# A graph network on one core: the adjacency stage and the gate stage joined in one loop, with one-hots used on chip and sums added up in PSUM

## What is computed

```python
# start of the first layer: the gate of each edge, and its sums by source node
gate = silu(edge_attr @ F1W + F1b) @ F2W + F2b
ei, ej = emb[atom_z[src]], emb[atom_z[dst]]
gate = gate + (ei * (ej @ adapt)).sum(-1, keepdims=True)
cw   = where(distances < CUT, 0.5 * (cos(pi * distances / CUT) + 1.0), 0.0)
mj   = node_mult[dst]
msg  = gate * h[dst] * (cw * mj)[:, None]
agg  = segment_sum(msg, src, num_segments=N)
tot  = clip(segment_sum(mj, src, num_segments=N), 1e-08, None)
h    = _ln(h + agg / tot[:, None], gn, bn)

# later: 5 and 10 steps of m = segment_sum(w * h[row], col)
```

## Time and profile before

| | us |
|---|---|
| median of 3 runs | 9919.12 |
| span of the profiled execution | 10065.2 |
| TensorE matmul busy | 7153.0 (71%) |
| VectorE busy | 6009.4 (60%) |
| GpSimd busy | 4708.2 (47%) |
| ScalarE busy | 3716.3 (37%) |
| stretch of the tables | 1490.0 to 1536.3 |
| adjacency stage | 1536.3 to 2928.4 |
| gate stage with its scans | 2996.7 to 3664.0 |

### The profile page before, as it was taken

How to read it: one execution, slowest core, us unless ns; L and a number is a source line. 1 busy time by engine, 2 the same in 40 slices (tenths; PEclk the granted TensorE clock), 3 DMA queues, 4 the chain that set the end, 5 groups by cost and what they waited for, 6 DMA issues and landing times. The chain is left out here.

```text
span 10065.2 us, 316920 instructions
## 1 busy us (share of the span) xinstructions
PE 7153.0 (71%) x106494; PEld 5756.9 (57%) x106495; DVE 6009.4 (60%) x18492; ACT 3716.3 (37%) x12956; POOL 4708.2 (47%) x6247
## 2 busy tenths in 40 slices
PE   2888865766657849976994998599578788833323
PEld 1555544555547749975994898499434344433323
DVE  6555558888867778997997899799700100011112
ACT  3222216777753326753662676377300000000000
POOL 0777770000016625542551554255267476556665
PEclk9999998888879979987996999799799899855555
DMA  8222224555439949965992997499488899611112
GB/s 330 60 61 61 62 52 162 192 186 188 136 103 308 310 137 255 263 178 147 261 261 65 262 263 205 121 262 263 128 333 334 322 365 364 236 29 18 18 18 19
DMA packets 1841808, 1846.73 MB, mean 183 GB/s; under 512 B 1462965, under 2 KB 1477717, under 8 KB 1796469
## 3 DMA queue, kind: packets, MB, share of 16 engines
q1 hardware_dynamic: 1727618, 1668.62, 54.0%
q0 software_dynamic: 112016, 153.10, 5.9%
q10 hardware_dynamic: 2016, 22.94, 0.6%
HBM read 1481.79 MB, written 360.62 MB: 183 GB/s over the span
## 5 line engine op out<-in xcount | busy, mean ns | idle before, releaser
L1649 POOL TENSOR_TENSOR s_rest<-s_msg 128x196 f32<-128x196 f32 x1488 | 762.6, 512 | 1881.7 <-ACT s_msg L1631 1819.4
L1239 PE MATMUL s_gotd<-m_table_d,s_hot 128*128 x17856 | 1363.2, 205 | 207.3 <-DMA s_hot<-OHT 195.2
L1631 ACT ACTIVATE s_msg<-s_gotd,s_es 128x49 f32<-128x49 f32 x5952 | 1304.4, 303 | 48.3 <-ACT s_es L1624 0.2
L1239 PE MATMUL s_gotq<-m_table_s,s_hot 128*128 x17856 | 1280.0, 185 | 7.1 <-issue 6.9
L1239 PEld LDWEIGHTS s_gotd<-m_table_d,s_hot 128*128 128x128 bf16 x17856 | 989.1, 96 | 291.4 <-DMA s_hot<-OHT 196.6
L1916 POOL DMA_INDIRECT REC<-m_sums x800 | 957.1, 1196 | 353.5 <-issue 346.8
L463 POOL DMA_INDIRECT REC<-rec,place x800 | 960.9, 1201 | 260.5 <-issue 228.5
L2195 POOL DMA_INDIRECT l_row<-H,l_rec x816 | 786.6, 964 | 501.3 <-issue 252.7
L1682 DVE TENSOR_REDUCE s_tops<-s_mt 128x512 f32 (+1 forms) x1488 | 1013.6, 681 | 6.5 <-PE s_mt L1592 6.3
L1949 PE MATMUL p_acc<-p_row,p_feats 128*64 128x512 f32 (+1 forms) x4032 | 900.2, 570 | 160.3 <-DMA p_row<-ADJ 157.3
L1239 PEld LDWEIGHTS s_gotq<-m_table_s,s_hot 128*128 128x128 bf16 x17856 | 992.1, 97 | 5.9 <-issue 5.9
(11 more groups left out here) (422 smaller groups left out, 18333.1 us busy)
## 6 DMA issues: line engine op xcount, KB each, us to landing
s_hot<-OHT SPq DMA_DIRECT2D x1488, 384.0 KB
p_row<-ADJ SPq DMA_DIRECT2D x288, 1600.0 KB
s_rec<-REC SPq DMA_DIRECT2D x1488, 98.0 KB
OHT<-a_turned SPq DMA_DIRECT2D x372, 384.0 KB
g_hot<-OHT SPq DMA_DIRECT2D x372, 384.0 KB
ADJ<-a_acc POOLq DMA_DIRECT2D x25, 3200.0 KB
REC<-fill SPq DMA_DIRECT2D x124, 624.0 KB, 10.2
g_rec<-REC SPq DMA_DIRECT2D x372, 108.0 KB
```

The lines of the kernel that those rows point to most:

```text
L1239: last = nc.tensor.matmul(out, hot, table[k][:, bass.ds(at, w)], start=(k == 0), stop=(k == 2))
L1631: last = nc.scalar.activation(msg[:, b % KEPT, j], gotd[b % KEPT][:, j, SW:2 * SW], ACT.Copy, scale=es[:, b % 2, j:j + 1])
L1649: nc.gpsimd.tensor_tensor(rest[:, b % KEPT].rearrange("p g w -> p (g w)"), msg[:, b % KEPT].rearrange("p g w -> p (g w)"), upper(msg[:, b ...
```

## The change

`adjacency` and `gate_pass` become one stage, `build_pass`, that runs after `start_nodes`. Each one-hot is made once, used for the products, the gathers and the sums while it is in SBUF, and still stored in `OHT` for attention; it is not read back.

- *Weights.* A record carries the weight as three bf16 parts that lie in two words, beside a 1.0. VectorE multiplies the destination one-hot by these words (`pieces`), so that one word array holds the one-hot, the high, the middle and the lowest part. All products of a tile are bf16: one of 256 columns (counts and high part), two of 128 (middle, lowest), the last two added in PSUM to the first. ScalarE's widening and weighting are gone.
- *Sums.* The destination blocks are taken in pairs (`UNITS`, 13 to a row). A pair's sums stay in one PSUM bank while its tiles go by, in a ring of four banks, and TensorE adds to them. A product of one column with zeros (`clear`) opens a bank or half a bank; where nothing is opened it is aimed at a spare place. In each group ScalarE moves two banks of 512 columns to `acc`, finished ones or, where there is none, into a spare place (`move_out`). The message sums too stay in one bank (`AGG`) over a source block, and ScalarE copies them to their place after each group. The scans are gone.
- *Banks.* Transposes have one bank instead of two, the gathers two instead of four, the message sums one instead of two.
- *Queues.* The loads of the records and the stores of the one-hots move from SP to ScalarE's queue, SP writes the rows of `ADJ`, which GpSimd did. The stores of `META` and `PLACE2` move from GpSimd's queue in the adjacency stage to SP's in `tile_tables`.
- *Registers.* ScalarE loads one and then four registers a group, TensorE four more than before and works out three addresses for each tile; VectorE loads none.
- *Tables.* `tile_tables` works out these places on 25 partitions and on one.
- *Sort.* GpSimd makes the parts of the weights in `sort_edges`, VectorE no longer copies the weight.

The core of the diff:

```diff
-CW, W, NORM, SL, DL, GIDX = 50, 51, 52, 53, 54, 55
+CW, HIGH, LOWEST, SL, DL, NORM, GIDX = 50, 51, 52, 53, 54, 55, 56
...
+                nc.gpsimd.tensor_tensor(thirds[:], wt[:], halves(wt[:], 1), ALU.subtract).then_inc(s_third, 1)
+                nc.gpsimd.tensor_copy(high[:, :, HIGH - CW, 1], halves(wt[:], 1)).then_inc(s_third, 1)
+                nc.gpsimd.memset(high[:, :, LOWEST - CW, 1], 1.0).then_inc(s_third, 1)
...
+                def take_turned(n, b, lap):
+                    act.wait_ge(s_ptr, n + 1)
+                    nc.scalar.copy(turned[:, b % TURNED, :, 0:2], ptr).then_inc(s_turned, 1)
...
+                def store_turned(n, b, lap):
+                    act.wait_ge(s_turned, n + 1)
...
+                def keep_sums(n, b, lap):
+                    sums_place(n, b, lap)
+                    act.wait_ge(s_agg, n + 1)
+                    nc.scalar.copy(sums_flat[:, bass.ds(at["sums", b], SW)], agg).then_inc(s_part, 1)
+
+                def move_out(n, b, lap):
+                    ways_out(n, b, lap)
+                    banks, units, kept = at[b]
+                    act.wait_ge(s_sums, n + 1)
+                    act.wait_ge(s_kept, kept)
+                    if past(n, 1):
+                        act.wait_ge(s_gone, n)
+                    act.sem_inc(s_load, 1)
+                    for k in range(2):
+                        last = nc.scalar.copy(
+                            acc[:, :, bass.ds(units[k], 1)].rearrange("p h o (d c) -> p h (o d) c", c=P),
+                            bank[:, bass.ds(banks[k], 1)].rearrange("p o (d h c) -> p h (o d) c", h=2, c=P))
+                    last.then_inc(s_gone, 1)
...
+                laps(act, [(load, 0), (take_turned, LEAD), (store_turned, LEAD), (keep_sums, LEAD + 4),
+                           (move_out, LEAD + 1), (embeddings, LEAD + 1)], SLOTS)
...
+                def owned(n, b, lap):
+
+                    if past(n, 1):
+                        pe.wait_ge(s_gone, n)
+                    if past(n, 2):
+                        pe.wait_ge(s_msg, n - 1)
...
+                def products(n, b, lap):
+                    for j in range(G):
+                        slot = pe.snap(lands[b][j] & 7).with_bounds(min_val=0, max_val=7)
+                        clear(pe.snap((lands[b][j] >> 3) & 15).with_bounds(min_val=0, max_val=2 * RING + 2))
+                        hot = turned[:, b % TURNED, j, 2]
+                        pieces = words[:, b % WORDS, j]
+                        nc.tensor.matmul(flat[:, bass.ds(slot * (2 * P), 2 * P)], hot,
+                                         upper(pieces.rearrange("p w c -> p (w c)")),
+                                         start=False, stop=False, skip_group_check=True)
...
+                laps(pe, [(own_offsets, 1), (turn, 0), (owned, 1), (add, 4), (products, 1), (addresses, 1),
+                          (gathers, 1), (offsets, 0)], SLOTS)
...
+                    for j in range(G):
+                        v.tensor_scalar(turned[:, b % TURNED, j, 2], mem["iota_bf"][:],
+                                        rec[:, b, j, SL - CW:SL - CW + 1], None, ALU.is_equal)
...
+                            last = v.tensor_scalar(words[:, b % WORDS, j, which], mem["iota"][:],
+                                                   rec[:, b, j, DL - CW:DL - CW + 1], rec[:, b, j, field:field + 1],
+                                                   ALU.is_equal, ALU.mult)
...
-                laps(dve, [(crossed, 0), (shifted, 1), (shifts, 0), (times_h, 1), (cut_off, 0)], SLOTS)
-                dve.wait_ge(s_part, NG)
-                ch = Chain(dve, s_dve)
-                add_groups(nc, dve, ch, mem, parts, mem["goes_on"][:])
+                v.memset(bank[:, AGG], 0.0).then_inc(s_clean, 1)
+                laps(dve, [(crossed, 4), (sources, 0), (shifts, 4), (pieces(0, range(G)), 0), (cut_off, 4),
+                           (pieces(1, range(2)), 0), (shifted, 4), (pieces(1, range(2, G)), 0), (times_h, 4)], SLOTS)
...
         start_nodes(nc, mem, io, tables)
-        gate_pass(nc, mem)
+        build_pass(nc, mem)
         after_gate(nc, mem)
```

552 lines of the change are left out of this document (310 added, 242 removed).

## The result

The changed kernel takes **10154.03 us** (median of 4 runs, 10151.46 to 10159.97) against 9920.06 us before, a ratio of 1.024 with a 95% interval of 1.0225 to 1.0254. It is 234 us slower. The forecast was 9690 us, with a range up to 9950: wrong in its sign, and outside its range.

The account below looks back on a forecast made before the run. VectorE's work and register loads limited the adjacency stage, DMA read-back the gate stage. With 4.83 us a group, 1812 (loop) + 8 (tables) + 4 (sort) - 2059.4 = -235 us, scaled to -232: 9690 us, range 9400 to 9950.

Parts of the forecast that it names:

- the sum headed *TensorE: TensorE's turn in the joined loop: 4.5 us a group at 2.4 GHz, 5.6 at 1.2 GHz, counted whole.
- The register arithmetic: 24 new TensorE instructions a group between the products, 0.07 us each: 1.6 us; half covered at 1.2 GHz.
- The clock: TensorE's granted clock in the joined loop: about 0.3 of the time at the lower level, granted 0.8 to 0.9.
- Rival A: Joined loop: TensorE becomes the bound at 1.2 GHz, register arithmetic mostly open, 6.0 us a group, 10116 us; chance 0.13.
- ScalarE's turn: ScalarE's stream in the joined loop: 4.2 us plus three hand-overs with TensorE at about 0.1, 4.5 us a group.
- Rival B: Joined loop: ScalarE pays register loads at 0.8 us and the records' load start, 5.5 us a group, 9935 us; chance 0.10.
- VectorE: Joined loop: 12 narrow comparisons, 1.7 us, and the gate's operations, 1.2 us: 2.9 us a group, not on the path.
- rival C: Joined loop: register loads are covered, VectorE and GpSimd set the pace at 3.9 us a group, 9347 us; chance 0.12.
- DMA: Joined loop: 707 KB a group at 301 GB/s is 2.4 us, costing nothing while a group takes longer.
- The late transfer: Joined loop: records might arrive late behind the 3200 KB rows, at most some 4 us in 25 rows, 100 us.
- Sort: `sort_edges`: GpSimd makes the weights' parts beside VectorE's preparation, + 4 us for the shared ports, bounds 0 and 8.
- What would show it: Signs if right: loop 1750 to 1850 us, ScalarE about 60%, VectorE 60 to 70%, DMA 0.6, clock 0.8 to 0.9, tables 50 to 60 us.

Follow-up runs that it names:

- the best version: Changed kernel with TensorE laps of 6, places as plain words, one ScalarE load, gate one turn earlier: 9844.07 us; then with one TensorE register load a group: 9766.70 us.
- fixed_places: Changed kernel with products aimed at fixed places, so TensorE's 24 register instructions a group go and the sums land wrongly: 9955.81 us, 1.0029.
- eight_more_products: Changed kernel with TensorE in laps of 6 (10050.39 us), plus eight products of 56 columns with zeros a group ahead of the gathers: 10052.17 us, 1.0127.
- all_of_it: Changed kernel with TensorE in laps of 6, places as plain words, and ScalarE's two register loads made one of six words: 9844.88 us, 0.9928.
- one_register_load: all_of_it with the gate one turn earlier (9844.07 us), and TensorE's two register loads a group made one of 12 words: 9766.70 us, 0.9842.
- one_load_hidden: Changed kernel with only ScalarE's two register loads a group made one of six plain words behind the copy of the transposes: 10109.81 us, 1.0192.
- plain_places: Changed kernel with places of sums as column numbers, 8 words a group instead of 4 packed, so 12 of 24 register instructions go: 9924.80 us, 1.0003.

## Why the prediction was wrong, point by point

- **The step that failed** is the sum headed *TensorE*: "At 2.4 GHz that makes 4.5", from which "0.7 x 4.5 + 0.3 x 5.6 = 4.83 us a group" follows. The turn measured 5.6 us at either clock. By stretches of a turn, forecast and measured (us; 35 turns at a granted clock of 0.90 or more, 62 at 1.2 GHz):

| from ... to | 2.4 GHz, forecast | measured | 1.2 GHz, forecast | measured |
|---|---|---|---|---|
| first transpose to first addition | 0.43 | 0.56 | 0.86 | 0.88 |
| first addition to first product | 0.41 | 0.62 | 0.61 | 0.53 |
| first product to first gather, with the register arithmetic | 2.88 | 2.94 | 3.01 | 2.70 |
| first gather to next transpose | 0.76 | 1.44 | 1.12 | 1.52 |
| turn | 4.5 | 5.6 | 5.6 | 5.6 |

- **Two register loads on TensorE** are what the last stretch lacked, 0.68 us at 2.4 GHz and 0.40 at 1.2. They were in no term: I had found them hidden in the gate stage and priced them on ScalarE alone. That the gap is theirs is shown by the run that moves them, with which it moves; one load fewer, in the best version, gained 0.21 us a group. The other 0.34 us at 2.4 GHz stand around the additions and weren't told apart.
- **The register arithmetic** was priced at 1.6 us a group at 2.4 GHz, 0.8 of it open at 1.2 GHz. Its stretch came out right at 2.4 and 0.3 too long at 1.2, and the runs without it agree: with 12 of the 24 gone the turn fell by about 0.5 us, with all gone by 0.7 to 0.8, where ScalarE's stream held it. At 1.2 GHz the term that was too long made up for the loads that were missing, so the 5.6 is right by luck.
- **The clock** was missed, 0.62 of the time at the lower level instead of 0.3, but in this loop it did not matter: both turns are 5.6 us. Where the register arithmetic is gone the two differ again: in fixed_places the 86 turns at 2.4 GHz took 4.5 us on average, the 14 at 1.2 GHz 5.8. From 4.83 to 5.57, the mean of the ordinary turns, is 0.74 us a group or 275 us.
- **What the sum lacked besides** is the reading again of TensorE's and ScalarE's loops. No row of before showed it, and I hadn't asked what the length of a loop costs. The runs without it gained 104 (TensorE), 55 or 44 (ScalarE) and 187 us (both), 0.50 us a group. The rows of `ADJ` are some 50 us more (below). With the first two laps, which are 24 us shorter than the others, this makes up the 476 us between the 1812 forecast for the loop and the 2288 measured, within some 15.
- **Rival A** had the right engine. Its 6.0 us and 10116 us are near 6.15 and 10154, but by a turn that is 0.4 too long, and without the pauses and the loads, so it came near through errors that offset. Its chance, 0.13, was low. The evidence against it, a clock of 0.85 in a stage with as many waits, was none: the joined loop had 0.69 with TensorE busy 77% of it instead of 68%, and the clock did not set the turn anyhow. eight_more_products shows only that more work in the gaps raises it.
- **ScalarE's turn**: forecast 4.5 us, measured 4.76 where it is the pace (fixed_places). The register loads were 0.77 and 1.09 us, between the 0.34 and the 0.8 of the prediction's bounds for the first, above them for the second with its arithmetic. The two copies of the banks took 1.07 (1.16 forecast), the start of the records' load nothing, as said. Rival B's 5.5 us for that stream was too long, and it was not the pace.
- **VectorE**: 1443.8 us, 3.9 us a group instead of 2.9. The comparisons with a product started 0.26 to 0.28 us apart, nearly twice the row they were priced by the earlier trace rows, which is a comparison with a constant and no more. It had cover: VectorE waited 452 us for TensorE's additions. VectorE's busy time alone is rival C's whole turn, but what ruled C out was TensorE's stream.
- **DMA**: priced at nothing; its share was 0.35, not 0.6. The late transfer does cost something: laps while rows of 3200 KB go out take 74.8 us on average, those after the last row 72.4, some 50 us in all. The prediction allowed 100, on VectorE; it shows up at ScalarE's register loads. In the changed kernel, where the store follows the copy directly, the store starts on time and the load of one register behind it stands 0.6 us longer than in other turns:

```profile
2373.61 0.51 SPq L1288 DMA_DIRECT2D ADJ<-b_acc  x1
```
```profile
2374.12 1.01 ACT L1304 COPY b_turned<-b_bank 128x1024 bf16<-128x1024 bf16 x1 [0.36 <-PE b_bank L1391]
2375.37 0.35 ACTq L1326 DMA_DIRECT2D OHT<-b_turned  x1
2376.85 0.20 ACT L1333 COPY m_sums<-b_bank 128x49 f32 x1 [1.72 <-issue]
```

  In all_of_it the load of six words stands between the copy and the store, and there the wait is 4.5 us:

```profile
2398.84 0.51 SPq L1299 DMA_DIRECT2D ADJ<-b_acc  x1
```
```profile
2400.29 1.01 ACT L1315 COPY b_turned<-b_bank 128x1024 bf16<-128x1024 bf16 x1 [1.31 <-PE b_bank L1403]
2405.88 0.35 ACTq L1338 DMA_DIRECT2D OHT<-b_turned  x1
2406.36 0.20 ACT L1346 COPY m_sums<-b_bank 128x49 f32 x1 [5.05 <-issue]
```

  The turn takes 7.5 us instead of 5, some 23 times, 55 to 60 us. Between copy and store it is 0.68 us in the median and up to 4.6 in the runs with the load there (all_of_it, one_register_load, up to 4.7 in one_load_hidden), and never above 0.6 in three runs without it (the changed kernel, fixed_places, plain_places). So it is the load that stands still, not the start of the store; why six words stand so much longer than one isn't shown. It was not tried to move or split these rows, or to put the load elsewhere.
- **Tables**: forecast + 8, measured + 5.2 (51.5 against 54 us in sum). Right.
- **Sort**: forecast + 4 with bounds 0 and 8, measured + 18.9, of which 14.7 stand ahead of the first scatter. The term took the shared ports for a small tax, and VectorE's operations stood still for whole operations of GpSimd. The Trainium skill, SBUF — State Buffer, section SBUF: two separate sides, has the rule: of an operation of VectorE that needs the shared port pair and one of GpSimd, whichever starts first keeps the pair for its whole instruction. The trace agrees, with 7.27 us for an operation of 0.58 that ends 0.4 us behind one of GpSimd's, as the next two do, and I had used that rule for the loop only.
- **What would show it**: of the six marks, loop time, DMA share and clock were missed, VectorE's share (63%) and the tables (51.5 us) were met, and ScalarE was busy 41% instead of 60%. "ScalarE waits mostly for TensorE's products" was named as the sign of A, and the waits show it: 342.1 us for the products and 334.2 for the transposes.
- **A slip in the range**: by the prediction's own sum a turn of 4.4 to 5.3 us is 9530 to 9860 us, not 9510 to 9840. Nothing hangs on it.

## What to carry to other kernels

When a stage is rewritten so that one engine gets places out of registers, sum up that engine's instructions of all kinds in the order of its stream, register loads included, and count the length of its loop in instructions: at 2.4 GHz the array's work was 2.6 of 5.6 us here, by the prediction's own sum of its steps, and a faster clock gave nothing back. Measure a turn from the same instruction to the same instruction of the engine that sets the pace; the takings of an engine that waits for it lie 4.9 to 6.3 us apart where the pace is 5.6. The same change pays (1.6% below the kernel before instead of 2.4% above it) once its tables hold finished column numbers, TensorE's loop is half as long, and the loads of registers are few. A wait names what ended last; before a ring is deepened for it, look at what stands right behind it in the waiting engine's own stream.

## What the runs showed of the hardware

- A loop on TensorE of 12 such groups is read again on every lap (q8: 5.82 MB instead of 1.54), at 5 to 8 us of standing still for each return in the timeline and 3.5 us net; one of 6 groups is not (1.51 MB), and 372 groups written out are read without loss that shows (5.06 MB). ScalarE's has the same at 12 groups (q14: 1.71 against 0.56 MB), 1.5 to 1.8 us net a lap.
- A turn of TensorE with 61 products, 24 register and address instructions between them and two register loads takes 5.6 us at 1.2 GHz (5.64, 62 turns) and at 2.4 GHz (5.58, 35 turns).
- More work on TensorE cost nothing there: 8 products a group in a gap raised the granted clock from 0.74 to 0.86, and the time stayed within 2 us.
- A register load on TensorE is not covered by the products queued ahead of it: moved between additions and products it cost 0.71 us a group more (10419 us), in the best version 0.24 (9856 against 9767 us).
- An operation of VectorE of 0.58 us takes up to 7.27 us beside GpSimd's operations on every other half-word.
- While a transfer of 3200 KB goes out, a load of one register on ScalarE stood 0.6 us longer, and a load of six words some 4 us longer (4.5 us from copy to store instead of 0.68).
